# Selecting each row's own window after the matmul, in a 4x4-window linear attention kernel on Trainium2

## The reference, cut to what matters

```
xw = x.reshape(B, C, Hn, ws, Wn, ws).transpose(0, 2, 4, 1, 3, 5)
qkv = jnp.einsum('nchw,oc->nohw', xw, qkv_w)
pooled = _avg_pool5(qkv)
msq = jnp.concatenate([qkv, pooled], axis=1)
...
q = relu(msq[..., :DIM]); k = relu(msq[..., DIM:2 * DIM]); v = msq[..., 2 * DIM:]
v = jnp.pad(v, (..., (0, 1)), constant_values=1.0)
kv = jnp.einsum('ngld,nglm->ngdm', k, v)
out = jnp.einsum('ngld,ngdm->nglm', q, kv)
out = out[..., :-1] / (out[..., -1:] + 1e-15)
...
y = jnp.einsum('nchw,oc->nohw', out, proj_w)          # then the batch norm
x = x + y                                             # x as it came in
```

## Time and profile before

| | us |
|---|---|
| median of three runs | 895.9 |
| the profiled execution | 900.88 |
| its span in the trace | 899.1 |
| TensorE busy | 859.1 (96%) |
| VectorE busy | 695.4 (77%) |
| GpSimd busy | 666.7 (74%) |
| ScalarE busy | 509.9 (57%) |

### The profile page before, as it was taken

The page is one execution under the profiler, slowest core; times in us unless marked ns, Lnnn a source line. Parts: engine busy times, 40 slices in busy tenths (PEclk is TensorE's granted clock), DMA queues, the critical chain, the costliest instruction groups (busy, mean ns, idle before and its releaser), DMA issues.

```text
span 899.1 us, 65691 instructions
## 1 busy us (share of the span) xinstructions
PE 859.1 (96%) x29282; PEld 740.6 (82%) x29282; DVE 695.4 (77%) x1236; ACT 509.9 (57%) x1350; POOL 666.7 (74%) x1641
## 2 busy tenths in 40 slices
PE   0789999999999999999999999999999999999996
PEld 0667888888888888888888888888888888888885
DVE  7466888888677888888776888888777777777775
ACT  0344656565655656565656556565656565565653
POOL 2666778777878777777878787777878787877772
PEclk9999999999999999999999999999999999999998
DMA  6122232111113232211113232211111111111111
GB/s 232 40 75 65 86 104 82 46 48 46 47 64 100 85 97 87 68 46 47 47 47 90 92 100 84 80 52 50 47 49 47 46 47 47 47 49 45 53 50 37
DMA packets 39082, 60.07 MB, mean 67 GB/s; under 512 B 8560, under 2 KB 33648, under 8 KB 39024
## 3 DMA queue, kind: packets, MB, share of 16 engines
q1 hardware_dynamic: 39024, 59.52, 19.7%
HBM read 19.38 MB, written 18.87 MB: 43 GB/s over the span
## 4 chain that ended last, share of the span: by engine, by line
PE 94%; DVE 2%; DMA 1%; issue 1%; SPq 0%; POOL 0%; ACT 0%; POOLq 0%; DVEq 0%
PE ps L630 23%; PE ps L615 17%; PE ps L587 15%; PE ps L597 9%; PE ps L603 9%; PE ps L704 7%; PE ps L695 6%; PE ps L706 4%; PE ps L604 4%; DVE stats L442 1%; DMA vm_full<-v_full 1%; DMA x_all<-x 1%; SPq L232 0%; DVE kvc_full L509 0%; POOL xn L287 0%
## 5 line engine op out<-in xcount | busy, mean ns | idle before, releaser
L357 ACT ACTIVATE vm_pool<-ps,cst 128x256 f32<-128x256 f32 x576 | 231.0, 481 | 5.1 <-PE ps L597 0.5
L367 ACT ACTIVATE q_full<-ps 128x384 f32<-128x384 f32 x96 | 47.3, 492 | 285.0 <-PE ps L603 285.0
L284 POOL TENSOR_TENSOR xd<-x_all,mean_t 128x384 f32<-128x384 f32 x96 | 79.5, 828 | 159.7 <-PE ps L604 143.0
L509 DVE TENSOR_TENSOR kvc_full<-ps,cst 128x864 f32<-128x864 f32 x192 | 193.2, 1048 | 5.2 <-PE ps L615 5.2
L509 DVE TENSOR_TENSOR kvc_pool<-ps,cst 128x864 f32<-128x864 f32 x192 | 193.1, 1047 | 1.4 <-PE ps L615 1.4
L587 PE MATMUL ps<-wkv_sb,xn 128*128 128x128 f32 x1152 | 146.4, 278 | 24.0 <-POOL xn L287 24.0
L587 PEld LDWEIGHTS ps<-wkv_sb,xn 128*128 128x128 f32 x1152 | 145.2, 194 | 24.0 <-issue 24.0
L262 POOL TENSOR_TENSOR x_all<-y_pool,x_all 128x96 f32<-128x96 f32 x384 | 150.8, 427 | 17.2 <-ACT y_pool L394 17.2
L287 POOL TENSOR_TENSOR xn<-xd,rstd_t 128x96 f32<-128x96 f32 x384 | 123.4, 369 | 7.5
L630 PEld LDWEIGHTS ps<-kvc_full,q_full 64*32 64x32 f32 x9216 | 108.0, 105 | 25.3 <-issue 25.2
L630 PE MATMUL ps<-kvc_full,q_full 64*32 64x72 f32 x9216 | 124.8, 230 | 0.0
(11 more groups left out here) (67 smaller groups left out, 1295.9 us busy)
## 6 DMA issues: line engine op xcount, KB each, us to landing
vm_full<-v_full SPq DMA_DIRECT2D x384, 54.0 KB, 1.9
out<-x_all SPq DMA_DIRECT2D x96, 192.0 KB, 1.9
x_all<-x SPq DMA_DIRECT2D x36, 384.0 KB, 3.5
x_all<-x SPq DMA_DIRECT2D x6, 768.0 KB, 8.1
cst<-consts SPq DMA_DIRECT2D x1, 170.0 KB, 11.0
wkv_sb<-wkv SPq DMA_DIRECT2D x1, 128.0 KB, 10.8
o_sb<-proj SPq DMA_DIRECT2D x1, 128.0 KB, 10.2
wq_sb<-wq SPq DMA_DIRECT2D x1, 64.0 KB, 10.5
```

What stands on the lines that cost most here:

```text
L284: link(pool.tensor_tensor(xd[:], x_all[:, s * SP:(s + 1) * SP], mean, ALU.subtract), 1)
L357: last = act.activation(heads[:, e, :, :, 0:D], src, ACT.Copy, scale=col(C_VP + e))
L509: last = dve.tensor_tensor(kvc[:, g], src.to_broadcast(shape), own, ALU.mult)
```

## The change

Each out product takes all windows of its block at once: 144 columns for the 2 full windows, 216 for the 3 pooled ones, 24 and 16 products to a strip. PSUM then holds, for every row, the result for each window of the block. ScalarE copies the first window's columns to a new tile (`sel_full`, `sel_pool`), and VectorE writes the others over it with `copy_predicated` where a constant mask (`C_WIN`) says that the row belongs to that window: one such copy for full, two for pooled. The division reads the new tiles, and `kv_products_pooled` waits for `sel_f` (the full selection) where it waited for `num_f`. k and v are convolved together, 256 columns to a product. The first strip is normalised on VectorE (`first_strip`) beside the second on GpSimd, `conv_kv` of strip 1 comes ahead of the first k-v products, and in the last strip the full out products come ahead of the projection and the last pooled addition is VectorE's.

```
+        def full_windows(bank):
+            return ps[:, bank:bank + G, 0:TF * WF * QG * KC].rearrange(
+                "p g (t e c) -> p g t e c", e=WF, c=QG * KC)
...
             def masked_v_pooled(s, between=None):
...
                 for e in range(EP):
                     last = act.activation(heads[:, e, :, :, 0:D], src, ACT.Copy, scale=col(C_VP + e))
                     if between is not None and e == 1:
                         copy_y_pooled(between)
+                    if e == 3 and s > 0:
+                        first_window(s - 1)
                 last.then_inc(vm_p, 1)
+                if s > 0:
+                    first_window_pooled(s - 1)
...
+            def first_window(s):
+                act.wait_ge(out_f, s + 1)
+                wait(act, num_f, s)
+                bank = OUTF_LAST if is_last(s) else OUTF
+                act.activation(sel_full[:], full_windows(bank)[:, :, :, 0], ACT.Copy).then_inc(win_f, 1)
...
             def divide(s, pooled):
...
-                dve.wait_ge(ready, s + 1)
-                src = ps[:, bank:bank + G, 0:tiles * QG * KC].rearrange("p g (n c) -> p g n c", c=HC)
+                if pooled:
+                    dve.wait_ge(win_p, s + 1)
+                    for e in range(1, WP):
+                        own = col(C_WIN + WF + e).bitcast(mybir.dt.uint32).unsqueeze(2).unsqueeze(3)
+                        dve.copy_predicated(sel_pool[:], own.to_broadcast([P, G, TP, QG * KC]),
+                                            pooled_windows()[:, :, :, e]).then_inc(sel_p, 1)
+                        dve.wait_ge(sel_p, (WP - 1) * s + e)
+                    src = sel_pool[:].rearrange("p g t (n c) -> p g (t n) c", c=HC)
+                else:
+                    dve.wait_ge(win_f, s + 1)
+                    own = col(C_WIN + 1).bitcast(mybir.dt.uint32).unsqueeze(2).unsqueeze(3)
+                    dve.copy_predicated(sel_full[:], own.to_broadcast([P, G, TF, QG * KC]),
+                                        full_windows(bank)[:, :, :, 1]).then_inc(sel_f, 1)
+                    dve.wait_ge(sel_f, s + 1)
+                    src = sel_full[:].rearrange("p g t (n c) -> p g (t n) c", c=HC)
...
             def conv_kv(s, p):
...
+                for t in range(TF):
+                    bank, at = KV_F + t // 2, t % 2 * 2 * P
+                    last = pe.matmul(ps[:, bank, at:at + 2 * P], xn[:, p, t * P:(t + 1) * P], wkv_sb[:],
+                                     start=True, stop=True)
+                last.then_inc(conv_f, 1)
...
+            def out_group_f(t, bank):
+                n = WF * QG * KC
                 for g in range(G):
                     rows = slice(H64 * g, H64 * (g + 1))
                     for c in range(4):
-                        r, w = c // QG, t * QG * wins + c % QG * wins + e
+                        r, w = c // QG, (t * QG + c % QG) * WF
                         last = pe.matmul(ps[Q4 * c:Q4 * (c + 1), bank + g, t * n:(t + 1) * n],
-                                         blocks[rows, 4 * t + c, Q4 * e:Q4 * (e + 1)], kvc[rows, r, w],
-                                         start=e == 0, stop=e == wins - 1)
+                                         q_full[rows, 4 * t + c], kvc_full[rows, r, w:w + WF],
+                                         start=True, stop=True)
...
             def kv_products_pooled(s):
                 pe.wait_ge(vm_p, s + 1)
-                wait(pe, num_f, s)
+                wait(pe, sel_f, s)
```

More of the change, by code:

```diff
@@ L594, in conv_kv_pooled @@
                 wait(pe, qm_p, s)
-                for half, bank, done in ((0, K_P, k_p), (1, V_P, v_p)):
-                    for t in range(TP):
-                        last = pe.matmul(ps[:, bank, t * P:(t + 1) * P], xp[:, p, t * P:(t + 1) * P],
-                                         wkv_sb[:, half * P:(half + 1) * P], start=True, stop=True)
-                    last.then_inc(done, 1)
+                for t in range(TP):
+                    last = pe.matmul(ps[:, KV_P, t * 2 * P:(t + 1) * 2 * P], xp[:, p, t * P:(t + 1) * P], wkv_sb[:],
+                                     start=True, stop=True)
+                last.then_inc(conv_p, 1)
             def conv_q(s, p):
@@ L628, in out_tile, with out_group_p @@
                     for c in range(4):
-                        r, w = c // QG, t * QG * wins + c % QG * wins + e
+                        r, w = c // QG, (t * QG + c % QG) * WF
                         last = pe.matmul(ps[Q4 * c:Q4 * (c + 1), bank + g, t * n:(t + 1) * n],
-                                         blocks[rows, 4 * t + c, Q4 * e:Q4 * (e + 1)], kvc[rows, r, w],
-                                         start=e == 0, stop=e == wins - 1)
+                                         q_full[rows, 4 * t + c], kvc_full[rows, r, w:w + WF],
+                                         start=True, stop=True)
+                return last
+            def out_group_p(t):
+                n = WP * QG * KC
+                for g in range(G):
+                    rows = slice(H64 * g, H64 * (g + 1))
+                    for c in range(4):
+                        r, w = c // QG, (t * QG + c % QG) * WP
+                        last = pe.matmul(ps[Q4 * c:Q4 * (c + 1), OUTP + g, t * n:(t + 1) * n],
+                                         q_pool[rows, 4 * t + c], kvc_pool[rows, r, w:w + WP],
+                                         start=True, stop=True)
                 return last
             def kv_products(s):
+                if isinstance(s, int) and s < 2:
+                    pe.wait_ge(km_f, s + 1)
                 pe.wait_ge(vm_f, 16 * EF * (s + 1))
@@ L654, in out_wait @@
                     pe.wait_ge(qm_p, s + 1)
-                pe.wait_ge(kvc_p, s + 1)
+                    pe.wait_ge(kvc_f, s + 1)
+                else:
+                    pe.wait_ge(kvc_p, s + 1)
             def out_products(s):
@@ L663, in out_products @@
                 for t in range(TF):
-                    for e in range(WF):
-                        last = out_tile(False, t, e)
+                    last = out_group_f(t, OUTF_LAST if is_last(s) else OUTF)
                 last.then_inc(out_f, 1)
@@ L678, in out_products_pooled @@
                 for t in range(TP):
-                    for e in range(WP):
-                        last = out_tile(True, t, e)
+                    last = out_group_p(t)
                 last.then_inc(out_p, 1)
@@ L693, in transposes @@
                         (TRF, o_full, TF, P, C_IDENT, tr_f), (TRP, o_pool, TP, 4 * WP * PXP, C_PACK, tr_p)):
+                    if is_last(s) and o is o_pool:
+                        pe.wait_ge(num_p, s + 1)
                     for t in range(n):
@@ L729, in _ @@
             last.then_inc(proj_turned, 1)
+            pe.wait_ge(v_copied, 1)
+            pe.wait_ge(km_f, 1)
+            conv_kv(1, 1)
             pe.wait_ge(projT_ready, 1)
```

163 lines of the change are left out of this document (116 added, 47 removed).

## The result

The changed kernel took 1098.89 us (median of 4 runs, 1098.5 to 1098.93), 1.2257 times the kernel before (95% interval 1.2236 to 1.2279). It is slower, as forecast, inside the range of 1005 to 1125, and 41 us above the 1058 of the likeliest case, whose own range of 1035 to 1085 it misses by 14.

A forecast was written before the change was run, and what follows sets the result against it. VectorE's chain, 0.15 us a strip under TensorE, was to take over: 8.70 + 0.37 (ScalarE's window) + 1.63 (selections) = 10.70 us; 36.8 + 94 periods (1005.8) + 19.8 + 1.8 = 1064.2, as a median 1058 us, range 1005 to 1125.

The forecast's parts named there:

- the likeliest case: Whole kernel: a period of 10.70 us a strip gives 1058 us, own range 1035 to 1085, chance 0.74.
- VectorE's circle: Chain from VectorE's divisions and own_heads through TensorE's projection and full out products back: would close in 8.70 us a strip.
- slack of 0.15 us: Per strip before the change: TensorE's period of 8.85 us was put only 0.15 us above the 8.70 of VectorE's chain.
- ScalarE's window: ScalarE's copy of the full first window, behind masked copies: VectorE starts at 2.93 us instead of 2.56, +0.37 a strip.
- Full copy: VectorE's predicated copy for the full windows, 432 elements: 0.61 us, 0.64 with its link.
- Pooled copies: VectorE's two predicated copies for the pooled windows, 288 elements each: 0.46 us each, 2 x 0.495 with links.
- Pooled division: VectorE's division of the pooled result: reading SBUF instead of PSUM afterwards was costed at 0.
- half a pass: Rival for VectorE's predicated copies: an element in half the time, 0.52 us less a strip, 1009 us; chance 0.06.
- two passes: Rival for VectorE's predicated copies: two passes over the elements, 1.04 us more a strip, 1156 us; chance 0.06.
- TensorE's own bound near 8.1: With merged products and wider convolutions, TensorE alone would need about 8.1 us a strip, against 8.85 before.
- The faster rival: TensorE stays the bound with selections nearly free: 8.1 us a strip, 812 us; chance 0.03, or 0.04 with no change.
- The rival of a falling clock: TensorE waits a quarter of the time and its clock falls: 1128 to 1199 us, say 1150; chance 0.10.

The follow-up runs named there:

- the first run: The changed kernel with the windows part taken back (72-column out products, division from PSUM), k and v side by side and reordered ends kept: 887.36 us, 0.9874 of the kernel before.

## Why the prediction was right, and where a size was off

**The bound.** Right: VectorE's circle stood close under TensorE and took over. The slack of 0.15 us was too large; one operation more showed 0.06 to 0.07. Most of the difference is a link: of the 0.20 us from `kvc_p` to the projection's weight load the prediction counted 0.05 as needed, but where TensorE really waits there it takes 0.11 (520.34 to 520.45). The rest is the period, read from one strip as 8.85 where the usual one is 8.82 to 8.83.

**The period.** Term by term, from the rows above: from `kvc_p` to VectorE's start behind ScalarE's window 2.96 us (0.11 to the weight load, and 512.27 + 11.03 - 520.45 = 2.85), forecast 0.05 + 2.93 = 2.98; that these agree is in part luck, as the one is 0.06 over and the other 0.08 under. Full copy 0.71 (forecast 0.64). Full division 1.20 (1.21). Pooled copies 1.02 (0.99). Pooled division 1.20, forecast 0.94: this is the term that failed, by 0.26. Both `own_heads` 3.94 (3.94). Sum 11.03 against 10.70. So of the 0.33 missing, 0.10 is the copies and 0.26 a division that I had costed at no change when its source moved from PSUM to SBUF. The run that keeps GpSimd still gave back 0.25 of it.

**The copies.** By form over the middle they took 657 and 476 ns, with 0.04 to the next. The trend of two-source rows gave 607 and 459; neither half a pass nor two passes. The formula of the Trainium skill (VectorE: DVE Perf Modes, the section on the TRN2 errata) had given an estimate of 575 and 425: lower still, and the measurement decides.

**ScalarE's window.** Right to 0.1 us, and the shorter out products were used up in it, as forecast.

**TensorE.** The merged full products took 0.99 us and start 0.76 ahead of the next: the merging gives what the k-v rows said. The "nothing" that the prediction drew from the rule of the Trainium skill (TensorEngine Tiling (Array Packing), Instruction Overhead) is refuted here. TensorE's own bound near 8.1 was not seen by itself; 8.57 less the DMA wait of 0.5 in the run without windows gives an estimate of 8.05. The faster rival lacked this DMA as a limit as well.

**The clock.** The rival of a falling clock didn't happen in the middle: the longest wait was 1.33 us and the granted clock of 200 to 1050 us was 1.00. It did fall at the end, where TensorE waits longest (2.93 us ahead of 1080.89): granted 0.79 from 1080 to 1084 us and 0.57 from 1088 to 1096; one projection took 1.65 us there (0.88 in the middle). In the kernel before it fell at the end too: granted 0.92 from 860 to 899 us, and a projection of 1.44 us. How much of the 3.2 us that the end took over the forecast is the clock's wasn't separated.

**The sum.** 36.09 for 36.8 (-0.7), 94 x 11.03 for 94 x 10.70 (+31.4), 23.0 for 19.8 (+3.2): 33.9 of span over the forecast of 1062.4. The rest of the 41 us is the scaling: I took 0.9945 from the profiled execution to the median, but here the profiled execution (1098.5) and the median (1098.89) agree, which accounts for 6 us. So the direction and the mechanism were forecast, and the likeliest case's own range was missed; the wider range holds the time by the room that it left for a clock that falls in some strips, which is not what happened.

## What to carry to other kernels

A page that shows one engine at 96% and the next at 77% can hide a second circle a tenth of a microsecond below; follow it once by its waits before moving work onto the second engine, and count as free only what stands outside that circle, not what fits the sum of the engine's pauses. Fewer, wider full out products took 0.33 us less from start to start, and picking the wanted rows afterwards cost 0.54 us of ScalarE and 1.73 of VectorE, all in the circle: leaving the selection in the matmul, with zeros in the stationary operand, was the cheap place. When an operand moves from PSUM to SBUF, look for what GpSimd does at that moment.

## What the runs showed of the hardware that I had not expected

**VectorE's work out of SBUF is slowed by GpSimd's.** A product of 256 elements with both sources in SBUF took 678 ns beside GpSimd's work and 426 without. Before, with one source in PSUM, it took 426 on average, though GpSimd was adding while it ran:

```profile
458.59 1.57 POOL L262 TENSOR_TENSOR x_all<-y_pool,x_all 128x96 f32<-128x96 f32 x4
...
459.45 0.42 DVE L528 TENSOR_TENSOR o_pool<-ps,den_pool 128x256 f32<-128x256 f32 x1
```

A one-source operation on 48 elements of SBUF took 0.47 us beside GpSimd's additions, against 0.20 with GpSimd idle (512.98). In the run without the copies `o_pool` was fast and a denominator slow, as their places had moved: in the usual strip the pooled one, first in the changed kernel, then in this run (minimum, median, maximum):

```profile
L638 DVE TENSOR_SCALAR den_pool<-sel_pool x96: 187/190/389, 40.9 to 1089.2; 128x32 f32<-128x32 f32 x96
```

```profile
L633 DVE TENSOR_SCALAR den_pool<-sel_pool x96: 170/374/415, 40.5 to 924.0; 128x32 f32<-128x32 f32 x96
```

and in some strips with `bn_stats`, as in this one, the full one:

```profile
505.34 0.50 DVE L633 TENSOR_SCALAR den_full<-sel_full 128x48 f32<-128x48 f32 x1 [1.28 <-ACT sel_full L426]
...
507.46 0.43 DVE L637 TENSOR_TENSOR o_pool<-sel_pool,den_pool 128x256 f32<-128x256 f32 x1
```

The reciprocals, which read SBUF too, weren't slowed: 353 ns for 32 elements in the changed kernel, beside GpSimd's `xd`, and 353 in the run that keeps GpSimd still. The Trainium skill (VectorE: DVE Perf Modes, in the section on two Vector instructions with no wait between them) says that the second of two SBUF inputs, or the input of an operation in a 2-port mode, comes through a read interface that VectorE shares with GpSimd. The two-source rows agree with it; whether the slowed denominators ran in such a mode no run here shows.

**TensorE stalls in the first strips.** With 96 small out products to a strip, TensorE stands still for some 2 us in the first three strips with no releaser that the profile shows; in the first run:

```profile
54.09 0.83 PE L714 MATMUL ps<-vm_full,k_full 64*32 64x144 f32 x38 [1.97 <-issue]
...
64.50 0.66 PE L729 MATMUL ps<-kvc_pool,q_pool 64*32 64x72 f32 x37 [1.93 <-issue]
```

The first three periods were 12.57, 10.63 and 14.59 us before and 12.61, 11.15 and 10.98 in the first run, but 11.14, 11.03 and 10.77 in the changed kernel, at its usual length. All six kernels with 96 small products have first periods of 10.5 to 14.6 us; in the other seven none is more than 1.1 us above the usual one. What TensorE waits for there wasn't tested and stays open.
